# Cross attention and mixture of experts: a program of its own for the first preparation

## What is computed

```
h = layernorm(x)
q     = rms_norm(h @ q_w.T + q_b) * norm_q_w              # 16 heads of 32
k     = rms_norm(ctx_txt @ k_w.T + k_b) * norm_k_w ;      v     = ctx_txt @ v_w.T + v_b
k_img = rms_norm(ctx_img @ k_img_w.T + k_img_b) * ... ;   v_img = ctx_img @ v_img_w.T + v_img_b
x = x + (attention(q, k, v) + attention(q, k_img, v_img)) @ o_w.T + o_b
g = softmax(layernorm(x) @ Wg + bg); the best 2 of 8 experts for each token, with their weights
x = x + sum over the two of weight * (gelu(gelu(y @ W1 + b1) @ W2 + b2) @ W3 + b3)
```

## Time and profile before

| | us |
|---|---|
| median of 3 runs | 876.22 |
| lowest, highest | 872.66, 877.42 |
| the profiled execution | 865.58 |
| its span in the trace | 863.8 |

### The profile page before, as it was taken

The page is one execution under the profiler, slowest core; times in us unless marked ns, Lnnn a source line. Parts: engine busy times, 40 slices in busy tenths (PEclk is TensorE's granted clock), DMA queues, the critical chain, the costliest instruction groups (busy, mean ns, idle before and its releaser), DMA issues.

```text
span 863.8 us, 17380 instructions
## 1 busy us (share of the span) xinstructions
PE 775.2 (90%) x5934; PEld 672.6 (78%) x5934; DVE 601.8 (70%) x1275; ACT 495.6 (57%) x1131; POOL 231.1 (27%) x286
## 2 busy tenths in 40 slices
PE   3889898989998999766499999999999999999993
PEld 2657676767776767444498999999999999999992
DVE  4476878787979787655575858676766757676863
ACT  4357777777777767685153645554545455464551
POOL 3232434343434343213460303030211203030300
PEclk9799999999999999775699999999999999999997
DMA  6641010202020100222795655556465565565540
GB/s 212 242 151 58 2 59 20 72 23 69 23 69 28 65 22 24 84 108 93 256 341 202 242 213 207 214 196 232 176 260 204 216 225 210 203 246 203 206 169 2
DMA packets 28209, 126.22 MB, mean 146 GB/s; under 512 B 4236, under 2 KB 4252, under 8 KB 17664
## 3 DMA queue, kind: packets, MB, share of 16 engines
q1 hardware_dynamic: 22544, 109.80, 35.6%
q0 software_dynamic: 5616, 15.81, 5.2%
HBM read 108.68 MB, written 19.01 MB: 148 GB/s over the span
## 4 chain that ended last, share of the span: by engine, by line
PE 67%; DVE 12%; ACT 8%; issue 5%; DMA 3%; POOL 3%; SPq 0%; POOLq 0%; ACTq 0%; DVEq 0%
PE tiles L1041 6%; PE tiles L1043 6%; PE tiles L1042 6%; PE scores L1304 4%; PE scores L1305 4%; PE scores L1303 4%; PE ptb L1151 4%; PE pvb L1043 3%; PE pvb L1042 3%; PE pvb L1041 3%; PE ptb L1043 3%; PE ptb L1042 3%; PE ptb L1041 3%; PE scores L1141 2%; PE pvb L1174 2%
## 5 line engine op out<-in xcount | busy, mean ns | idle before, releaser
L830 DVE TENSOR_TENSOR w<-scr,w 128x2048 fp32r<-128x2048 f32 x75 | 170.8, 2288 | 61.6 <-ACT w L620 61.6
L620 ACT ACTIVATE w<-scr 128x2048 fp32r<-128x2048 f32 x76 | 144.9, 1909 | 60.8 <-PE scores L1305 60.8
L473 POOL DMA_INDIRECT out_dram<-scr,tok x18 | 19.4, 1079 | 311.4 <-DVE scr L1027 308.7
L602 ACT ACTIVATE scr<-scr,rsum 112x257 f32<-112x257 f32 x128 | 66.5, 520 | 62.4 <-DVE rsum L814 62.4
L1041 PE MATMUL tiles<-c,w 128*128 128x256 f32 (+1 forms) x272 | 82.4, 303 | 18.3 <-DVE c L718 15.7
L1041 PE MATMUL tiles<-w 128*128 128x256 f32 x288 | 83.3, 289 | 0.9 <-DVE w L1017 0.2
L1015 DVE CAST w<-scr 128x256 fp32r<-128x256 f32 x144 | 43.8, 304 | 54.6 <-ACT scr L686 54.6
L1042 PE MATMUL tiles<-w 128*128 128x256 f32 x288 | 81.5, 283 | 0.0
L1043 PE MATMUL tiles<-w 128*128 128x256 f32 x288 | 81.4, 283 | 0.0
L1151 PE MATMUL ptb<-ident,scr 112*128 112x112 f32 x384 | 64.7, 280 | 18.3 <-ACT scr L610 16.6
L1042 PE MATMUL tiles<-c,w 128*128 128x256 f32 (+1 forms) x272 | 79.4, 292 | 0.0
(11 more groups left out here) (214 smaller groups left out, 2315.1 us busy)
## 6 DMA issues: line engine op xcount, KB each, us to landing
scr<-in_dram SPq DMA_DIRECT2D x82, 1024.0 KB, 4.8
scr<-in_dram SPq DMA_DIRECT2D x8, 750.0 KB, 4.5
scr<-slots_d SPq DMA_DIRECT2D x10, 528.0 KB, 5.5
slots_d<-rows SPq DMA_DIRECT2D x8, 528.0 KB, 11.6
xn<-in_dram SPq DMA_DIRECT2D x9, 256.0 KB
xb<-in_dram SPq DMA_DIRECT2D x8, 224.0 KB, 2.6
xr<-in_dram SPq DMA_DIRECT2D x8, 224.0 KB, 2.5
out_dram<-x SPq DMA_DIRECT2D x8, 224.0 KB, 2.7
```

The lines of the kernel that those rows point to most:

```text
L602: act.activation(probs[0:L, s, 0:IMG], probs[0:L, s, 0:IMG], ACT.Copy, scale=rsum[0:L, g, s, 0:1]).then_inc(S["normal_img"], 1)
L620: act.activation(EH[slot], raw[slot], ACT.Copy).then_inc(S["eh_done"], 1)
L830: dve.tensor_tensor(EL[slot], raw[slot], EH[slot].bitcast(F32), ALU.subtract).then_inc(S["el_done"], 1)
```

## The change

Body -1 is taken out of the loop: `bodies` begins at FIRST = 0, and each engine gets a function `first()` with the first preparation in an order of its own: xT, qt, kt (with q inside), k0, kx, k1, k2, k3, v0, v1 (ms inside), rb, v2. x is loaded first, then WQ, the context, WK, WKI, WVI, WV, in halves of the columns and into three buffers. GpSimd makes the high half of the first context. WO is split in quarters within body 0, through `x1` and a part of `rows` as buffers. The values of the last image keys are made within body 0, at h = 0 behind the first scores; their row is stored from `xr`. GpSimd's four small loads come behind the context's split. GpSimd writes the token's number and adds to the running counts, within `scatter`. The diff, cut:

```
-ORDER = (WKI, WK, WQ, WVI, WV, WO)
-WEIGHTS_AT = {2: 2, 7: 3, 11: 4, 15: 5}
+ORDER = (WQ, WK, WKI, WVI, WV)
+BIG_FIRST = ("qt", "kt", "k0", "k1", "k2", "k3", "v0", "v1", "v2")
+OUT_HIGH_AT = {1: 0, 2: 1, 8: 2, 9: 3}
+OUT_LOW_AT = {2: 0, 3: 1, 9: 2, 10: 3}
...
-        vlast = rows[0:B, 0, 0:D]
+        vlast = xr[0:B, :]
...
-        raw_w = [scr[:, probs_at + i * PIECE:probs_at + (i + 1) * PIECE] for i in range(2)]
+        raw_w = [scr[:, i:i + PIECE] for i in (probs_at, probs_at + PIECE, 0)]
+        raw_o = [x1[:, :], rows[:, 0, 0:D]]
...
+            def load_weights(i):                    # SyncE
+                for k in range(2):
+                    if i >= 3:
+                        sp.wait_ge(S["wh_done"], 2 * (i - 3) + k + 1)
+                        sp.wait_ge(S["wl_done"], 2 * (i - 3) + k + 1)
+                    sp.dma_start(side(raw_w[i % 3], k), side(wT[ORDER[i]], k)).then_inc(wraw_in[i % 3][k], 16)
...
+            sp.dma_start(xb[0:L, :], x[0]).then_inc(S["x_in"], 16)
+            load_weights(0)
+            sp.dma_start(cr, ctxT[0]).then_inc(S["c_in"], 16)
+            for i in range(1, 5):
+                load_weights(i)
+                if i == 2:
+                    sp.dma_start(xlT[:, :, :], ctx_last).then_inc(S["xl_in"], 16)
+            next_x(-1)
+            next_context(-1)
+            sp.wait_ge(S["zeroed"], 1)
+            load_out_weight(0)
+            load_out_weight(1)
+            for e in range(E):
+                sp.dma_start(slots_d[...], ...).then_inc(S["zero_stored"], 16)
...
+                    if fixed(b, FIRST):
+                        sp.wait_ge(S["vlast_sb"], 1)
+                        sp.dma_start(vlast_d, vlast).then_inc(S["vlast_out"], 16)
+                        sp.wait_ge(S["vlast_out"], 16)
...
+                    if fixed(b, FIRST):             # behind next_x(0), next_context(0)
+                        load_out_weight(2)
+                        load_out_weight(3)
...
             def scatter(r):                         # GpSimd
+                pool.wait_ge(S["lg_max"], r + 1)
+                pool.tensor_copy(rows[0:L, r % 2, D:D + 1].bitcast(U32), ids[0:L, r:r + 1]).then_inc(S["id_set"], 1)
+                pool.wait_ge(S["rank_ready"], r + 1)
+                pool.tensor_tensor(sofar[0:L, :], sofar[0:L, :], msk[0:L, :], ALU.add).then_inc(S["g_sofar"], 1)
+                pool.wait_ge(S["id_set"], r + 1)
...
+            def first():                            # GpSimd
+                rstd(1, mv1, ve1, rs1, "ln1")
+                pool.wait_ge(S["c_in"], 16)
+                for i in range(2):
+                    pool.tensor_copy(c_part(cH)[i], cr[:, :, PARTS[i]]).then_inc(...)
+                (four pool.dma_start of o_b, wg, bg, b12)
+                for name in ("q", "k0", "kx", "k1", "k2", "k3"):
+                    square(name, -1, 1)
+                rms_power(-1)
+                rstd(2, mv1, ve1, rs1, "ln1")
+                split_queries(0, 0)
+                split_keys(0, 0, 0)
+                split_ctx_high(1, 0)
...
+            def first():                            # ScalarE; split_weights(i, k) is half k of matrix i
+                split_weights(0, 0), (0, 1); evacuate("xT")
+                split_weights(1, 0), (1, 1); evacuate("qt")
+                split_weights(2, 0), (2, 1); evacuate("kt")
+                split_weights(3, 0); evacuate("k0"); split_weights(3, 1); evacuate("k1")
+                (high half of xlT); evacuate("k2"); split_weights(4, 0); evacuate("k3")
+                split_weights(4, 1); evacuate("v0"); evacuate("rb"); evacuate("v1")
...
+            def first():                            # VectorE
+                ln_stats(1, ...); split_weights(0, 0); ln_apply(1, ...); split_weights(0, 1)
+                take_x(-1); split_ctx_low(1, 0), (1, 1)
+                split_weights(1, 0), (1, 1), (2, 0), (2, 1)
+                take_q(-1, 1); split_weights(3, 0); take_kx(-1, 1); split_weights(3, 1)
+                (low half of xlT); split_weights(4, 0), (4, 1)
+                add_squares(-1, 0), (-1, 1); add_sums(-1); take_ms(-1)
+                (two memsets); ln_stats(2, ...); normalise_queries(-1, 1); normalise_keys(0, 0)
+                split_queries_low(0, 0); split_keys_low(0, 0, 0); normalise_keys(0, 1)
+                ln_apply(2, ...); split_ctx_low(2, 0)
...
-                dve.tensor_copy(rows[0:L, r % 2, D:D + 1].bitcast(U32), ids[0:L, r:r + 1])
...
+                if r:
+                    dve.wait_ge(S["g_sofar"], r)
                 dve.tensor_tensor(msk[0:L, :], sel[0:L, 0, :], sel[0:L, 1, :], ALU.add).then_inc(S["g_mask"], 1)
...
-                dve.tensor_tensor(sofar[0:L, :], sofar[0:L, :], msk[0:L, :], ALU.add).then_inc(S["g_sofar"], 1)
...
+                    if h == 0 and fixed(b, FIRST):  # TensorE, behind score(0, 0, 0), ahead of k0
+                        values_of_last_image_keys()
...
+            def first():                            # TensorE; the waits are for both halves of a matrix
+                stage("xT", 0, 1, -1, 1)
+                pe.wait_ge(S["wl_done"], 2)
+                stage("qt", 0, NC, -1, 1)
+                pe.wait_ge(S["wl_done"], 4)
+                stage("kt", 0, 2, -1, 1); stage("q", 0, 1, -1, 1); stage("kt", 2, NC, -1, 1)
+                pe.wait_ge(S["wl_done"], 6)
+                stage("k0", 0, NC, -1, 1); stage("kx", 0, 1, -1, 1); (k1, k2, k3 whole)
+                pe.wait_ge(S["wl_done"], 8)
+                stage("v0", 0, NC, -1, 1); stage("v1", 0, 2, -1, 1); stage("ms", 0, 1, -1, 1)
+                stage("v1", 2, NC, -1, 1); stage("rb", 0, 1, -1, 1)
+                pe.wait_ge(S["wl_done"], 10)
+                stage("v2", 0, NC, -1, 1)
```

231 lines of the change are left out of this document (144 added, 87 removed).

## The result

The changed kernel took **869.21 us** (median of 7 runs, 867.49 to 870.03), the kernel before 875.69 us in the same comparison (7 runs, 872.1 to 877.42): a ratio of 0.9939, 95% interval 0.9924 to 0.9955. The gain is 5.3 us by the ratio, 6.5 by the medians, where 13.0 were forecast. The profiled execution of the changed kernel took 869.21 us with a span of 867.4.

What follows compares the result with a forecast made beforehand. TensorE, busy 90% of the span, was taken as the bound, so the gain lay ahead of the first scores: 15.0 - 0.8 - 1.2 = 13.0 us off the median 876.22 gives 863.2, range 860 to 866.

Steps and rivals of the forecast that it cites:

- 15.0 us earlier: Opening: the new order of loads and preparation brings the first scores to 37.5 instead of 52.5 us.
- The first body gives back about 1.2 us beyond the 0.8: First body: VectorE's later maxima cost 0.8 us, and the work moved in costs about 1.2 more.
- The maxima's lag: First body: VectorE reaches the first maxima 2.7 us after the scores start, before 1.9, so 0.8 us back.
- The last keys' matmuls: First body: twelve matmuls, 2.8 us on TensorE, fill a gap behind the first scores; counted as 1 to 1.5 us.
- the cover is there: First body: idle time of ScalarE and VectorE hides WO's quarters and a copy; without it up to 2.5 us.
- -0.1 to +0.3: After the last rank: moving the token column and running counts to GpSimd shifts TensorE's wait this much; taken as 0.
- The median is 10.6 above the profile, the same 13 come off it: Whole kernel: the runs' median 876.22 exceeds the profile's 865.58; the same 13 us off give 863.2.
- Less: Opening, rival at 18%: GpSimd's casts blocked, WKI late, half loads slower; first scores 41 to 43, gain 7 to 10, 868.
- Given back in the first body: First body, rival at 5%: matmuls, ScalarE, VectorE and a late quarter add up to 11.6 us; gain 2.6, 873.6.
- Halves pay the fixed part: Opening loads, rival at 4%: each half load shows the full 1.48 us, costing 7.4; gain 5.6, 870.6.
- more: Opening and first body, rival at 20%: half-rate stretches return to full clock; gain 16 to 17 us, 859.5.
- Slower: Bodies, rival at 3%: shifted stalls fall into more half-rate clock stretches, up to 1.75 us each; 879.

Runs made afterwards that it cites:

- e3_two_buffers: Changed kernel with two buffers instead of three for the first weights, halves kept: 866.62 us in one run, against 873.79 for the kernel before.
- e3_best: Changed kernel with the last image keys' matmuls back in the preparation and the counts back on VectorE: 867.32 us, ratio 0.993 to the kernel before.
- e2_counts_on_vector: Changed kernel with the token column and running counts back on VectorE: 853.6 us in one run.
- e4_after: Changed kernel, unedited, on one more chip, with the long first expert block: 869.88 us, ratio 0.9956 to the kernel before.
- e2_after: Changed kernel, unedited, on a chip with the short first expert block: 853.81 us, ratio 0.9910 to the kernel before.

## Why the prediction was wrong

The time that I gave, 863.2, missed by 6 us, and the gain by more than half: 13.0 forecast, 5.3 measured (7.8 and 3.8 in the two later comparisons). By the profiles, over all those of each kernel with its own order of work:

| | kernel before | changed | forecast |
|---|---|---|---|
| first scores | 47.4 to 52.5, mean 50.3 (6) | 39.5 to 40.6, mean 39.8 (6) | 52.5 to 37.5 |
| first body | 40.9 to 41.7, mean 41.3 (6) | 43.8 to 45.1, mean 44.6 (6) | + 2.0 |
| rest of the bodies | 318.2 to 321.7, mean 319.2 (5) | 320.8 to 323.6, mean 321.9 (6) | 0 |

The lead is 10.5 where the sum has 15.0, the first body gives back 3.3 where it has 2.0, and the rest 2.7 where it has 0: 4.5 us are left, inside the measured 3.8 to 7.8. (The kernel before with the counts moved stands in the first two rows and not in the third.)

- **"15.0 us earlier" failed twice.** *Where it starts from:* 52.5 was one execution. I counted "about 4.5 half-rate time" into the gain as if every run of the kernel before paid it; three of six profiles had first scores at 47.4 to 50.6. That is 2.2 us of the 15. *Where it ends:* 37.5 became 39.8. In the profile after, with 40.64, two thirds of the slip of 3.1 are at the start: the first query matmul at 11.79 and not 9.7. ScalarE began on the first half of WQ at 6.51 instead of 5.0, so x was normalised at 9.28 instead of 7.7, and from there to the matmul the transposes, ScalarE, the additions took 2.5 instead of 2.0. From there on the steps held to within 0.4: queries out after 5.5 us (forecast 5.1; as forecast the 512-column matmuls come 0.43 us apart, where those of v0 come 0.23 apart, though the clock column reads 1.00 there), PE's stall 0.64 (0.6), the four key stages and kx 6.3 (6.3), values to broadcast 7.3 (7.1), broadcast to scores 5.8 (5.4).
- **"The first body gives back about 1.2 us beyond the 0.8."** The maxima's lag was sized right (2.34 us after the scores in this profile, 2.7 forecast). The last keys' matmuls, costed at 1 to 1.5, cost 0.35 at full clock and 1.0 with the half-rate stretch beside them: the forecast was right in kind, they fill a gap. What failed is "the cover is there": the four quarters, costed at 0, cost 0.6 us in the gap of the third and fourth, 0.8 more where ScalarE waits 2.1 us for the load (also costed at 0), and what is left in the first gap, 10.43 against 9.40 without the matmuls, of which the maxima's lag is about 0.5. At full clock in the first and third gap that makes 43.76 against 40.94, 2.8 us where the forecast has 2.0. The rest of the mean's 3.3 is half-rate time, which no term of the sum holds: four of the six changed profiles have 6.8 us of it between the second and third groups, the kernel before 3.5 in all six.
- **The counts, "-0.1 to +0.3", "I take 0".** 0.7 us are shown at the last rank alone. Over the bodies the means say more: with the counts on VectorE the changed kernel's rest is 320.1 (four profiles) against 321.9 (six), 1.9 us. But the ranges nearly meet (319.5 to 320.4, 320.8 to 323.6, and 320.2 in e3_two_buffers with the counts on GpSimd), and the time of e3_best and e2_counts_on_vector shows no gain. So a cost of 0.7 us is shown, and one of about 2 is likely but mixed with half-rate time. I looked at who waits for the addition, but not at what stands ahead of it in GpSimd's queue there: a memset behind a DMA. VectorE's 16 small operations, some 2.6 us and the reason for the move, bought nothing that a run shows.
- **"The median is 10.6 above the profile, the same 13 come off it."** The constant held for a reason that I didn't know. The profile had the short first block (39.70), and the runs beside it by their times the long one; as far as the medians show, both kernels share it, and it drops out.
- **Rivals.** "Less" (first scores at 41 to 43, gain 7 to 10, 868) came nearest in the time, through another mix: its ScalarE part is right (two buffers do as well as three), its late loads are not, and the gain was below it. "Given back in the first body" was right in kind and took 3.3 of its 11.6 us. "Halves pay the fixed part" was refuted and "more" never seen. "Slower" was never near, but what it named, half-rate stretches that move, is in the first body's loss. Its 879 is not what its terms give: ten stretches at 1.75 are 17.5 us, 4.5 more than the gain, 880.7.
- **Luck.** The three misses go the same way, so none hides another. The profile that I started from was the slowest opening of six, which was bad luck of 2.2 us: with the mean (50.3) the same steps would have forecast a gain of 10.8.
- **What stood the test.** Zero stores, the last keys' row, the small loads of GpSimd: no wait for them in the first 95 us of any profile. The quarters of WO were split at 0.63 us a piece on ScalarE and 0.69 on VectorE, not 0.48 and 0.57. The value row's issues were a bad measure of the first body, since the first of them now stands behind the last keys' store.

## What to carry to other kernels

A lead taken from one profile contains that execution's clock: take the busy time at full clock, or several profiles, before subtracting, and compare stretches of like clock when a change is set back. Work moved into a body costs little on the engine that waits there (0.35 us for 2.8 us of matmuls) and more on the two that feed it (0.6 us and up for two quarters), so "this engine is idle 13 of 43 us" is no cover by itself. An operation moved to an idle engine waits for what is queued there, so read that queue at the one place where someone waits for it. When medians stand 10 us off the profile, ask which stage has two lengths; here that was worth more than the change.

## What was not expected of the hardware

- **A burst of indirect stores can starve TensorE, on some chips.** Sixteen stores from GpSimd, back to back: the first block lasted 53.9 to 54.4 us in the profiles of three comparisons (unedited stores, whatever else was changed), and 39.4 to 40.6 in those of three others and in the kernel before's first profile. The stores' issue differs too; the long block (e4_after), then the short one (e2_after):

```profile
L476 POOL DMA_INDIRECT slots_d<-rows,fillu x16: 967/971/1023, 413.5 to 432.7; - x16
```

```profile
L476 POOL DMA_INDIRECT slots_d<-rows,fillu x16: 967/1058/1899, 414.7 to 437.2; - x16
```

  Where TensorE and VectorE go on working, the stores take up to 1.9 us each (minimum, median, maximum in ns); where they stand, 0.97 evenly. The Trainium skill, "SBUF — State Buffer", section "SBUF: two separate sides", warns that an operation of VectorE's in a two-port mode holds up a DMA whose descriptors GpSimd writes. The rows show a hold-up beside another kind of operation too, subtractions of two SBUF tiles. In e2_after, two of them and a store that took 1.90 us instead of 0.97:

```profile
425.34 4.49 DVE L894 TENSOR_TENSOR w<-scr,w 128x2048 fp32r<-128x2048 f32 x2
...
426.57 1.90 POOL L476 DMA_INDIRECT slots_d<-rows,fillu  x1 [0.30 <-issue]
```

  It would be tempting to say that this wider spacing saves the short block. The rows speak against it: up to where TensorE begins to stand in e4_after (424.35), the stores are spaced alike in both, the first to the ninth in 10.28 us (413.48 to 423.76) with the long block and in 10.47 (414.67 to 425.14) with the short one. The stretched stores follow from the work that goes on, and what tells the chips apart stays open.
- **The clock's half-rate stretches move an opening by 5 us between executions of one kernel** (52.52 and 47.44 us to the first scores, clock 0.85 and 1.00 over the same matmuls). The changed kernel's openings differ by 1.1 (39.50 to 40.64), and only half of that is clock: the slower one has the first half of WQ 0.5 us later (6.51 against 5.97), and its query matmuls come 0.43 us apart up to 17.0 us instead of 15.2.
- **A subtraction on VectorE is stretched beside a cast on GpSimd.** The low half of the keys took 1.36 us on VectorE beside GpSimd's cast of the context (1.89), in both kernels; the same line takes 0.54 us in the median.
